# Moving the router's transposes and logits of a cross-attention stage into the batches

## The reference, cut to what matters

```
q, k, v = norm(x) @ Wq, norm(ctx) @ Wk, norm(ctx) @ Wv     # 16 heads of 64
x = normalised(x + softmax(q k^T / 8) v @ Wo)              # per batch
logits = x @ Wr + br                                       # router: 256 -> 8, float32
probs = softmax(logits); two experts of eight are chosen for each token
```

## Time and profile before

| what | us |
|---|---|
| runs | 2250.69, 2253.78, 2245.33 |
| median | 2250.69 |
| profiled execution | 2256.79 |
| its span, first to last instruction | 2255.1 |
| TensorE busy in the span | 2176.0 |
| VectorE, ScalarE, GpSimd busy | 1505.9, 1361.9, 760.9 |
| mean granted TensorE clock | 0.981 of full |

### The profile page before, as it was taken

How to read it: one execution, slowest core, us unless ns; L and a number is a source line. 1 busy time by engine, 2 the same in 40 slices (tenths; PEclk the granted TensorE clock), 3 DMA queues, 4 the chain that set the end, 5 groups by cost and what they waited for, 6 DMA issues and landing times. The chain is left out here.

```text
span 2255.1 us, 57833 instructions
## 1 busy us (share of the span) xinstructions
PE 2176.0 (96%) x20778; PEld 1665.9 (74%) x20778; DVE 1505.9 (67%) x4396; ACT 1361.9 (60%) x3178; POOL 760.9 (34%) x1335
## 2 busy tenths in 40 slices
PE   7999999999998999999999999999999999989997
PEld 4776876867867677777777777777777777878876
DVE  4555545455447687777778787777777777376547
ACT  6546456356355576767767676767676767455434
POOL 1211221222215244544545454545454544100003
PEclk9999999999999999999999999999999999699988
DMA  5000000000001100000000000000000000052202
GB/s 162 20 1 1 0 0 0 0 0 0 15 19 39 42 10 16 11 16 11 16 10 16 10 17 10 16 10 17 10 16 10 16 3 2 1 141 85 75 1 66
DMA packets 45732, 51.44 MB, mean 23 GB/s; under 512 B 19120, under 2 KB 37664, under 8 KB 45504
## 3 DMA queue, kind: packets, MB, share of 16 engines
q1 hardware_dynamic: 45504, 48.45, 7.3%
HBM read 44.78 MB, written 3.67 MB: 21 GB/s over the span
## 5 line engine op out<-in xcount | busy, mean ns | idle before, releaser
L1744 POOL TENSOR_SCALAR arena<-arena,p_rec 112x375 f32<-112x375 f32 x512 | 303.0, 593 | 572.6 <-DVE p_rec L1607 569.2
L1611 DVE TENSOR_TENSOR pt_lo<-b_t,pt_hi 125x336 f16<-125x336 f32 x512 | 258.5, 505 | 234.7 <-ACT pt_hi L1502 234.5
L64 PE MATMUL b_pb<-arena 128*125 128x512 f16 (+1 forms) x1364 | 385.1, 303 | 14.1 <-ACT arena L1454 5.7
L65 PE MATMUL b_pb<-arena 128*125 128x512 f16 (+1 forms) x1364 | 377.7, 298 | 0.0
L66 PE MATMUL b_pb<-arena 128*125 128x512 f16 (+1 forms) x1364 | 377.4, 297 | 0.0
L1496 ACT ACTIVATE arena<-arena,neg_max 112x375 f32<-112x375 f32 x512 | 312.3, 610 | 1.6 <-DVE neg_max L1593 1.6
L1593 DVE CUSTOM_DVE_ANT_0 arena<-b_s,arena 112x375 f32<-112x375 f32 x512 | 273.5, 534 | 11.6 <-PE b_s L1353 6.8
L1362 PEld LDWEIGHTS b_t<-ident,arena 112*125 112x125 f32 x1536 | 237.3, 190 | 37.5 <-issue 1.4
L1362 PE MATMUL b_t<-ident,arena 112*125 112x112 f32 x1536 | 252.1, 273 | 0.0
L1502 ACT ACTIVATE pt_hi<-b_t 125x336 f16<-125x336 f32 x512 | 228.3, 446 | 6.0 <-PE b_t L1362 5.9
L64 PEld LDWEIGHTS b_pb<-arena 128*125 128x125 f16 (+1 forms) x1364 | 147.3, 108 | 95.7 <-issue 27.1
(11 more groups left out here) (284 smaller groups left out, 5717.3 us busy)
## 6 DMA issues: line engine op xcount, KB each, us to landing
arena<-in_L_ffn_W_dram SPq DMA_DIRECT2D x16, 1024.0 KB, 7.4
arena<-in_ctx_dram SPq DMA_DIRECT2D x32, 375.0 KB
out_dram<-c_z SPq DMA_DIRECT2D x8, 448.0 KB, 3.2
x_sb<-in_x_dram SPq DMA_DIRECT2D x1, 3136.0 KB, 18.8
ff<-in_L_attn_w_dram SPq DMA_DIRECT2D x2, 1024.0 KB, 7.6
ff<-in_L_xattn_Wkv_dram SPq DMA_DIRECT2D x2, 1024.0 KB, 5.4
arena<-in_mask_BxS_bf_dram SPq DMA_DIRECT2D x32, 41.0 KB, 2.6
a_raw<-in_L_attn_wq_dram SPq DMA_DIRECT2D x1, 1024.0 KB, 5.3
```

Source lines behind the costliest of these rows:

```text
L64: pe.matmul(out, lh, rh, start=first, stop=False)
L65: pe.matmul(out, lh, rl, start=False, stop=False)
L1611: dve.tensor_tensor(pt_lo[:, (H * b + h) % NPT, :], t_ps[h % 2][0:JP, 0:JT * T], pt_hi[:, (H * b + h) % NPT, :], ALU.subtract).then_inc(pt ...
L1744: pool.tensor_scalar(p32[:, h % 4, :], p32[:, h % 4, :], p_rec[:, h % 4:h % 4 + 1], 0.0, ALU.mult, ALU.add).then_inc(p_norm_done, 1)
```

## The change

The router's work moves from the last batch into the batches 1 to 31: batch b turns the rows of batch b-1 in step 12, after the weighted values, makes their logits in step 13, and adds the bias in step 14. One batch is routed at a time in place of two: two transposes and two logits matmuls (four records). ScalarE's copy of the turned columns stands in step 12 between turned_high and split_high_row. The uses RT and RL enter the ring of three banks behind the pieces of step 12 and 13 in every batch from 1 on. SP loads wr and br before the contexts of batch 2 and later.

```diff
+        ROUTE_AT = 12
         def body_uses(b):
             for s in range(H):
                 if not is_last(b):
                     uses.append(("P", b + 1, s))
-                else:
-                    if s > 0:
-                        uses.append(("RL", s - 1, 0))
-                    uses.append(("RT", s, 0))
                 if s == W_AT and not is_first(b):
                     uses.append(("W", b - 1, 0))
+                if not is_first(b):
+                    uses += [(kind, b - 1, 0) for kind, at in (("RT", ROUTE_AT), ("RL", ROUTE_AT + 1)) if s == at]
                 if has_prep(b):
                     uses += [(kind, b + 2, at.index(s)) for kind, at in (("X", X_AT), ("C", C_AT)) if s in at]
             if is_last(b):
-                uses += [("RL", H - 1, 0), ("W", b, 0)]
+                uses.append(("W", b, 0))
...
         # sync
+            sp.dma_start(wr[:, :, :], a["L0_ffn_Wr"].rearrange("(k p) e -> p k e", p=P)).then_inc(router_loaded, 16)
+            sp.dma_start(br[:, :], a["L0_ffn_br"].partition_broadcast(T)).then_inc(router_loaded, 16)
             for n in range(HEADED, B):
                 load(n, n % 2)
-            sp.dma_start(wr[:, :, :], a["L0_ffn_Wr"].rearrange("(k p) e -> p k e", p=P)).then_inc(router_loaded, 16)
-            sp.dma_start(br[:, :], a["L0_ffn_br"].partition_broadcast(T)).then_inc(router_loaded, 16)
...
         # tensor
+            def route_turn(b):
+                pe.wait_ge(x_done, b + 1)
+                ps = claim(use_number["RT", b, 0])
+                for k in range(KD):
+                    mm = pe.transpose(ps[:, k * T:(k + 1) * T], x_sb[:, b, k * P:(k + 1) * P], ident[0:T, 0:T])
                 mm.then_inc(pb_ready, 1)
+            def route_logits(b):
+                turned = use_number["RT", b, 0]
                 pe.wait_ge(free_of(turned), freed(turned))
+                if is_first(b):
+                    pe.wait_ge(router_loaded, 32)
+                ps = claim(use_number["RL", b, 0])
+                for k in range(KD):
+                    mm = pe.matmul(ps[0:T, 0:E], xr[:, b % 2, k * T:(k + 1) * T], wr[:, k, :], start=(k == 0), stop=(k == KD - 1))
                 mm.then_inc(pb_ready, 1)
...
             def body(b, par):
                     turn_scores(b, s)
-                    if is_last(b):
-                        if s > 0:
-                            route_logits(s - 1)
-                        route_turn(s)
...
                     if s == W_AT and not is_first(b):
                         out_rows(b - 1)
+                    if s == ROUTE_AT and not is_first(b):
+                        route_turn(b - 1)
+                    if s == ROUTE_AT + 1 and not is_first(b):
+                        route_logits(b - 1)
                     if has_prep(b):
                         if s in X_AT:
                             turn_x(b + 2, X_AT.index(s))
...
         # scalar
+            def route_columns(b):
+                use = use_number["RT", b, 0]
                 act.wait_ge(pb_ready, ready(use))
+                act.activation(xr[:, b % 2, 0:KD * T], bank(use)[:, 0:KD * T], ACT.Identity).then_inc(free_of(use), 1)
...
                     turned_high(b, s)
-                    if is_last(b):
-                        route_columns(s)
+                    if s == ROUTE_AT and not is_first(b):
+                        route_columns(b - 1)
                     if s == SPLIT_O_AT and is_first(b):
                         split_high("o")
                     if s == SPLIT_X_AT and not is_first(b):
                         split_high_row(b - 1)
...
         # vector
                         piece_low(b, par, NCH - 1)
-                    if is_last(b) and s >= 2:
-                        route_bias(s - 2)
+                    if s == ROUTE_AT + 2 and not is_first(b):
+                        route_bias(b - 1)
```

More of the change, by code:

```diff
@@ L1210, in body_uses @@
             if is_last(b):
-                uses += [("RL", H - 1, 0), ("W", b, 0)]
+                uses.append(("W", b, 0))
             return uses
-        def routed(s):
-            return range(2 * s, min(2 * s + 2, B - 1))
         def is_first(b):
@@ L1391, in out_rows @@
                 mm.then_inc(pb_ready, 1)
[L1393 to L1399, removed]
+            def route_turn(b):
[3 more added lines that the diff above has]
+                    mm = pe.transpose(ps[:, k * T:(k + 1) * T], x_sb[:, b, k * P:(k + 1) * P], ident[0:T, 0:T])
                 mm.then_inc(pb_ready, 1)
-            def route_logits(s):
-                turned = use_number["RT", s, 0]
+            def route_logits(b):
+                turned = use_number["RT", b, 0]
                 pe.wait_ge(free_of(turned), freed(turned))
[L1405 to L1410, removed]
+                if is_first(b):
[3 more added lines that the diff above has]
+                    mm = pe.matmul(ps[0:T, 0:E], xr[:, b % 2, k * T:(k + 1) * T], wr[:, k, :], start=(k == 0), stop=(k == KD - 1))
                 mm.then_inc(pb_ready, 1)
@@ L1442, in _ @@
             batches(body)
-            route_logits(H - 1)
             for h in (H - 4, H - 2):
@@ L1477, in piece_high @@
                 ins.then_inc(piece_hi, 1)
-            def route_columns(s):
-                use = use_number["RT", s, 0]
+            def route_columns(b):
+                use = use_number["RT", b, 0]
                 act.wait_ge(pb_ready, ready(use))
[L1482 to L1485, removed]
+                act.activation(xr[:, b % 2, 0:KD * T], bank(use)[:, 0:KD * T], ACT.Identity).then_inc(free_of(use), 1)
             def split_high_row(b):
@@ L1594, in mask_max, with route_bias @@
                                          ALU.add, ALU.min, neg_max[:, h % 4:h % 4 + 1]).then_inc(s_masked, 1)
-            def route_bias(s):
-                use = use_number["RL", s, 0]
-                if s == 0:
+            def route_bias(b):
+                use = use_number["RL", b, 0]
+                if is_first(b):
                     dve.wait_ge(router_loaded, 32)
                 dve.wait_ge(pb_ready, ready(use))
-                n = len(routed(s))
-                dve.tensor_tensor(logits[:, routed(s)[0]:routed(s)[-1] + 1, :], bank(use)[0:T, 0:n * E].rearrange("p (b e) -> p b e", e=E),
-                                  br[:, :].unsqueeze(1).to_broadcast([T, n, E]), ALU.add).then_inc(free_of(use), 1)
+                dve.tensor_tensor(logits[:, b, :], bank(use)[0:T, 0:E], br[:, :], ALU.add).then_inc(free_of(use), 1)
             def sum_reciprocal(b, h):
@@ L1685, in _ @@
             batches(body)
-            for s in range(H - 2, H):
-                route_bias(s)
             out_low(B - 1, 1)
```

## The result

The changed kernel takes 2330.43 us (median of 5 runs, 2326.19 to 2336.70) beside 2250.01 us for the kernel before on the same chip: a ratio of 1.0355, 95% interval 1.0339 to 1.0372. It is 80 us slower; 2335 was predicted, within 2295 to 2375.

The account below looks back on a forecast made before the run. TensorE, busy 96% of the span, was taken as the bound. 96.9 + 0.6 + 1.2 + 13 - 27 = 84.7 us on 2256.8 gave 2341.5; the median, 6.1 lower, 2335 us, range 2295 to 2375.

Parts of the forecast that it names:

- First wait: Step 13: TensorE's piece P13 waits 1.47 us for the context's bank, freed by ctx_columns behind the copy; 0.21 us work.
- Second wait: Step 14: P14 takes P13's own bank and waits 1.30 us for VectorE's piece_low, plus 0.36 us of logits.
- Per batch: Batches 1 to 29: 3.34 us longer each from both waits and the moved work, 96.9 us in all.
- Last batch: Last batch: 27 us saved on TensorE without the router's work, bounds 19 and 32.
- the upper bound: Last batch: saving of at most 32 us, as without the logits TensorE may keep the full clock longer.
- Start of the stage: Start of second stage: wr and br issued before batch 2's context make VectorE wait 1.2 us, between 0 and 1.9.
- the ceiling of 0.93 us for the issue of br: SP at the stage's start: issuing br, smaller than wr, cannot well take more than wr's 0.93 us.
- Clock in the batches: Steps 13 and 14: clock falls in a quarter of the batches, 1.7 us each, 13 us; bounds 0 and 49.
- 49 as a rival: Batches: clock falls in every one, 49 us in place of 13, 2371 us in all; chance 0.13.
- the stretches of 0.50 that were named as a sign: Some batches: stretches at clock 0.50 would show the forecast right.
- one wait would be absorbed: Batches: ScalarE or VectorE reaches a freeing instruction earlier, so one of the two waits goes; 2286 us; chance 0.11.
- The one that ended faster: Batches: banks come as early as before, only 0.57 us of work each; 2237 us; chance 0.05.

Follow-up runs that it names:

- Variant 1: The changed kernel with ScalarE's copy of the turned columns placed behind ctx_columns in step 12; 2283.7 us, 1.0129 of the kernel before.
- Variant 2: The changed kernel with the logits of batch b-2 in step 6 of batch b, in place of b-1 in step 13; 2289.8 us, ratio 1.0161.
- variant 3: The changed kernel with turns of batch b-2 in step 6 and logits in step 7; last batch routes 29 there, 30 in steps 12 and 13; 2246.6 us.
- variant 4: The changed kernel without turns, copies, logits and bias of batches 0 to 30 (logits set to zero, result not computed); 2226.0 us, ratio 0.9880.
- variant 6: The kernel before without its logits and their bias (logits zero, result not computed), turns and copies kept in the last batch; 2230.9 us, ratio 0.9898.
- variant 9: The kernel before with two unread matmuls of 256 float16 columns ahead of each group of logits in the last batch; 2242.1 us, ratio 0.9950.
- variant 5: The changed kernel routing batches 0 to 17 in steps 6 and 7 two batches later, 18 to 30 in the last batch, one per step; 2253.5 us.

## Why the prediction was right, point by point

- **First wait.** 0.21 us of work and 1.47 of wait were forecast, the latter on ctx_columns; the weight loads waited 1.5 us for it, 29 times, 1.31 us of it seen from the matmul. Variant 1 took it away and gave 1.48 us a batch. Right in place, count and size.
- **Second wait.** P14 was to start 3.04 us after P13, and did to the hundredth; the weight loads waited 38.2 us for it in 29 batches, 1.3 each. Variant 2 took it away and gave 1.31 us a batch, for 1.30 forecast.
- **Per batch** 3.34 us forecast, 3.43 measured (40.62 - 37.19); over 29 batches 99 us for 96.9. The work alone is 0.55 us by variant 3, for 0.57.
- **Last batch.** 27 us forecast with bounds 19 and 32, 29.3 measured. The size is luck, since it was made up otherwise: 9.2 us for turns (7 x 0.42 + 8 x 0.78), 16.6 for logits (7 x 0.72 + 8 x 1.45) and 1.2 for a single batch. Of these 8.7 us were clock; what half clock does to the rest of the batch stood in the upper bound alone. Variants 4 and 6 show that without the logits the turns cost nothing there (40.2 us with them, 40.4 without), and that leaving out the logits alone gives 29.4 us, of which 18 are more than their work and at least 13, by variant 9, come with the clock.
- **Start of the stage.** 1.2 us forecast, 5.9 measured. VectorE's first use of a context waited 1.83 us in place of 0.78, 1.05 more:

```profile
778.54 0.43 DVE L1540 BATCH_NORM_STATS2 arena<-arena 125x6 f32<-125x256 f32 x1 [1.83 <-DMA arena<-in_ctx_dram]
```

  The rest was in no term. Here the stretch from the issue of Wo to split_high_row in batch 1, before, after, and in variant 4, which moves the loads of wr and br too but routes nothing:

```profile
757.92:829.39 71.47, 66.86 (x689) 48.47 (x689) 54.60 (x176) 50.16 (x131) 30.82 (x56) 0.98 0.12 40
```

```profile
769.04:846.39 77.35, 71.59 (x727) 51.76 (x727) 56.28 (x181) 50.79 (x132) 31.79 (x57) 0.93 0.12 37
```

```profile
762.63:836.37 73.74, 69.44 (x689) 49.79 (x689) 55.05 (x177) 50.30 (x130) 30.81 (x56) 0.93 0.13 39
```

  In all eight profiles with the two loads moved the mean clock of this stretch is 0.93 and it takes 73.7 to 77.4 us; in the four with the loads where they were it is 0.98, and 71.5 to 71.8 us. So 2.3 of the 5.9 us go with the moved loads. 1.8 are the later place of split_high_row itself, behind the copy (variant 1, with the copy last, has 75.57). The remaining 1.8 differ between executions: variants 3 and 5, alike up to batch 17, have 73.86 and 75.47. Why the clock falls with the moved loads is not shown. Nor was the ceiling of 0.93 us for the issue of br safe: it took 0.46 us here, but 2.19 in variant 4.
- **Clock in the batches.** This is the term that failed. 13 us were taken for falls in a quarter of the batches, with 49 as a rival; the windows of the batches show 1.00 throughout, with both waits in every one, and the stretches of 0.50 that were named as a sign did not come. Beside the kernel before it fell further at the start of the second stage alone, where it had a part in the 5.9 us. What the Trainium skill (TensorE: Matmul & The Clock Gate, "A second HAM failure mode: psum-queue depth-cycling") reports of another kernel, a clock that swings because TensorE idles briefly while it goes through its banks, spoke for the 49 us. In this ring it did not come true: two bank waits of 1.3 to 1.5 us in each of 29 batches left the clock at 1.00. A longer one did not always: behind the wait of batch 0, which both kernels have, the matmuls of the changed one run at half clock, 0.43 us from start to start for 0.22 at full clock:

```profile
808.42 0.66 PE L64 MATMUL b_pb<-arena 128*125 128x512 f16 x1 [1.85 <-DVE k_lo L1566]
808.87 0.63 PE L65 MATMUL b_pb<-arena 128*125 128x512 f16 x1
```

  In the last batch of the kernel before it fell while TensorE was hardly waiting and made thin matmuls; in that of the changed kernel it is 0.75 in the last 13.5 us, in which TensorE is busy for 8.3 and makes only one batch's logits.
- **The rivals.** That one wait would be absorbed (2286 us) is refuted by the 3.43 us of a batch and by variants 1 and 2, which each give about what their wait was. The one that ended faster needed waits under 0.36 us a batch; variant 3 is that case, with 0.55 us of work, and came to 2246.6, where 2237 to 2242 had been worked out.

The sum was 84.7 us against 79.9 in the profiled execution and 80.4 between medians. Without its 13 us of clock it was 71.7; the second stage by itself lost 76.0 (5.9 + 96.1 + 3.3 - 29.3), and 3.9 came from the stages that the change doesn't touch. So the wrong term was partly covered by others on the other side, 4.7 at the start of the stage, 2.5 in the batches and 3.9 in code that the change doesn't touch, less 2.9 for the last batch and the one before. The two waits were foreseen by their mechanism; that the sum comes within 5 us is luck.

What stays open: why the clock falls at the start of the second stage with the loads moved, and why it falls at other places in the first stage from one execution to the next. The latter moved the start of the second stage between 757.9 and 774.9 us in the twelve profiles, with the same code ahead of it.

## What to carry to other kernels

Before a use is put into a ring of shared banks, write down for each use behind it whose bank it now takes and who frees that, and when; two new uses turned a distance of two pieces (P12 to P14) into one, and a copy placed ahead of the one that frees a bank held it for 1.5 us. In a stage where one engine has no slack, the price is that wait times the number of rounds, while the end of the kernel from which the work was taken pays back once. And thin float32 matmuls in a stretch with little other matrix work cost more than their own time, for the greater part because of the clock: spread them among dense work, or put dense work beside them.

## What the runs showed that had not been expected

That filler pays: 32 matmuls whose result nobody reads made the kernel 0.5% faster (0.9924 to 0.9975), by keeping the granted clock at 1.00 through the first 41 us of the last window, where it had held for 23. (The kernel before has such matmuls in its third stage, line 1919, but none here.) And that short waits were milder to the clock here than thin work: the changed kernel's batches, with TensorE idle for 2.9 of 40.62 us, kept 1.00, while the old last batch, busy for 64.0 of 69.6 us, had 0.71.
